# The product of (tanh + 1) with the gated value in layer 2 goes from VectorE to GpSimd, as a product and one more sum

## The chip, the cores and the metric

The kernel runs on one core of a Trainium2 chip. The metric is the device time of one execution in microseconds (us). In the profile PE is the matmul side of TensorE and PEld its weight loads, DVE is VectorE, ACT is ScalarE, POOL is GpSimd and SP is SyncE, which only issues transfers here.

## The reference, cut to what matters

Two layers run one after the other over 2048 tokens of width 256. Each adds s * silu(f) to the residual x. In layer 1 (index 0 in the reference) s is an attention and f a mixture of 64 experts; in layer 2 (index 1) s is an attention and f two ternary projections:

```python
x = L0_attn_q
xn = _layernorm(x)
s = _L0_attn_ref(xn, ...)
g = _silu(_L0_ffn_ref(xn, ...))
x = x + s * g
xn = _layernorm(x)
s = _L1_attn_ref(xn, ...)
g = _silu(_L1_ffn_ref(xn, ...))
x = x + s * g
```

The change touches the first `x = x + s * g`. The kernel computes silu(a) as a/2 * (tanh(a/2) + 1), with the factor of one half already in s. So with s0 = s/2 and a = the output of the experts, the sum is x + (tanh(a/2) + 1) * (s0 * a).

## The kernel before, in words

Tokens lie 128 to a tile, 16 tiles in all. The first 305 us are layer 1: the routing, the experts and its attention. Then a transfer brings the experts' sums back (`acc_ld`), and a software pipeline runs layer 2. It works on 8 pairs of tiles (NP = 8, GT = 2 tiles to a pair), and pair p holds tiles p and p + 8. A tensor of a pair is 128 partitions by 512 values.

Every engine runs a loop `for p in range(-AHEAD, NP)` with AHEAD = 3, and its instructions execute in the order written. In turn p of the loop the stages work on different pairs:

- pair p + 3: the end of layer 1. GpSimd adds the two halves of the experts' sum (`total`, L482) and multiplies s0 by it (`gated`, L488). ScalarE takes the tanh (`gate`, L685) into `tg`. VectorE forms (tg + 1) * s0 (`silu`, L1053). GpSimd adds that to x (`add_gated`, L493).
- pair p + 2: the layer norm. VectorE takes the moments (`moments`, L1060 to L1069). GpSimd raises the variances to the power -0.5 (`roots`, L513), for several pairs at once. VectorE mends these by a Newton step (`newton`, L1045 to L1047: three small instructions, each waiting for the one ahead) and normalises (`normalise`, L1081, two instructions, then L1083 and L1086).
- pair p + 1: the first projections and the gelu. TensorE multiplies (`fc` L1475, `qkv` L1462), ScalarE runs gelu, copy and square (`hidden`, L709, L716, L722; four times a turn), and VectorE forms the low half of the gelu's output (`low`, L1121, four times a turn) and that of x (`low_x`, L1091).
- pair p: the last projection and the sum. VectorE reduces the squares (`sum_squares`, L1128) and takes the spreads (`spreads`, L1134 to L1137, which feed `roots`), then scales (`half_scale`, L1145). TensorE multiplies (`down1`, L1508, which may start once `silu2` of the pair before has emptied its PSUM banks, and `square_sums`, L1515). ScalarE takes a tanh (`gate2`, L747), VectorE forms `silu2` (L1153) and `attended` (L1162), and GpSimd adds to x (`finish`, L507).

VectorE's order within a turn is: low_x, sum_squares, moments, spreads, low 0, newton, half_scale, normalise, products, low 1, score_difference, silu2, silu, low 2, attended, low 3. GpSimd's is: weigh, total, gated, roots, add_gated, finish. After `roots` has ended, VectorE's `newton` is released, and GpSimd goes on to `add_gated`. Turns p = -3 to -1 fill the pipeline, and the last turn with an `add_gated` is p = 4.

GpSimd's and VectorE's helper `then` issues an instruction and waits for its end on the same engine.

Of the kernel before, what the change touches and what calls it, by code (L numbers as in the profile page):

```python
# [10 lines left out]
ALU = mybir.AluOpType  # L11
# [42 lines left out]
NP = NT // 2  # L54
# [16 lines left out]
AHEAD = 3  # L71
# [6 lines left out]
def build(nc, q, router, Wkv, Wo, shared, sd, wgu_d, wdn_d, wqkv, wpo, wpo4, wfc, wpj, out):  # L78
# [9 lines left out]
    with ExitStack() as ctx:  # L88
        def sb(name, shape, dt=F32):
            return ctx.enter_context(nc.sbuf_tensor(name, shape, dt))  # L90

        def sem(name):
            return ctx.enter_context(nc.semaphore(name))
# [7 lines left out]
        x = sb("x", [P, NT, D])  # L101
# [61 lines left out]
        s0 = A[:, 4096:8192].rearrange("p (t d) -> p t d", t=NT)  # L163
# [33 lines left out]
        def l1(n):  # L197
            at[0] += n
            assert at[0] <= 10752, at
            return F[:, at[0] - n:at[0]]  # L200
# [8 lines left out]
        tg = [l1(GT * D).rearrange("p (s d) -> p s d", s=2) for _ in range(2)]  # L209
# [66 lines left out]
        acc_ready, gated_ready, gate_ready, silu_ready, x1_ready, xh_ready, xT1_ps, xT_hi_ready, xT_lo_ready = [  # L276
            sem(n) for n in ("acc_ready", "gated_ready", "gate_ready", "silu_ready", "x1_ready", "xh_ready", "xT1_ps",
                             "xT_hi_ready", "xT_lo_ready")]
# [10 lines left out]
        def pair(a, p):  # L289

            return a.rearrange("p (s i) d -> p s i d", s=2)[:, :, p, :]
# [105 lines left out]
        def _(pool):  # L397
# [91 lines left out]

            def add_gated(p):  # L490

                pool.wait_ge(silu_ready, p + 1)
                pool.tensor_tensor(pair(x, p), pair(x, p), tg[p % 2], ALU.add).then_inc(x1_ready, 1)  # L493

            def weigh(p):
# [275 lines left out]
        def _(ve):  # L771
            step = [0]

            def mark(ins):
                step[0] += 1
                ins.then_inc(dve, 1)
                return step[0]

            def then(ins):
                ve.wait_ge(dve, mark(ins))  # L780
# [259 lines left out]
            def newton(p):  # L1040

                c = root_cols(p)
                v, y, t_ = nv[:, c], ny[:, c], nt2[:, c]
                ve.wait_ge(root_ready, p + 3)
                then(ve.tensor_tensor(t_, y, y, ALU.mult))  # L1045
                then(ve.scalar_tensor_tensor(out=t_, in0=t_, scalar=-0.5, in1=v, op0=ALU.mult, op1=ALU.mult))
                then(ve.scalar_tensor_tensor(out=y, in0=t_, scalar=1.5, in1=y, op0=ALU.add, op1=ALU.mult))  # L1047

            def silu(p):

                ve.wait_ge(gate_ready, p + 1)
                ve.wait_ge(gated_ready, p + 1)
                ve.scalar_tensor_tensor(out=tg[p % 2], in0=tg[p % 2], scalar=1.0, in1=pair(s0, p), op0=ALU.add, op1=ALU.mult)\  # L1053
                    .then_inc(silu_ready, 1)

            def moments(p):

                ve.wait_ge(x1_ready, p + 1)
                for q_ in range(GT):
                    last = mark(ve.bn_stats(st1[:, q_, :], x[:, p + NP * q_, :]))  # L1060
                ve.wait_ge(dve, last)
                for q_ in range(GT):
                    last = mark(ve.bn_aggr(mv1[:, q_, :], st1[:, q_, :]))
                ve.wait_ge(dve, last)

                var = mv1[:, :, 1]
                mark(ve.tensor_scalar(nv[:, 0:GT], var, EPS_LN, None, ALU.add))
                ve.wait_ge(dve, step[0])
                ins = ve.tensor_scalar(nv[:, GT:2 * GT], var, 1.0 + EPS_Q, EPS_Q * EPS_LN, ALU.mult, ALU.add)  # L1069
                if p < 2:  # L1070
                    ins.then_inc(v_in, 1)
                    ve.wait_ge(v_in, p + 1)
                else:
                    then(ins)

            def normalise(p):

                if p >= 2:
                    ve.wait_ge(xT1_ps, p - 1)
                for q_ in range(GT):  # L1080
                    ve.tensor_scalar(xh[p % 2][:, q_, :], x[:, p + NP * q_, :], mv1[:, q_, 0:1], ny[:, GT + q_:GT + q_ + 1],  # L1081
                                     ALU.subtract, ALU.mult).then_inc(xh_ready, 1)
                then(ve.tensor_tensor(ratio[:, :], nv[:, GT:2 * GT], ny[:, GT:2 * GT], ALU.mult))  # L1083
                if p >= 2:
                    ve.wait_ge(kv_ready1, p - 1)
                ve.scalar_tensor_tensor(out=kvscale[p % 2][:, :], in0=ny[:, 0:GT], scalar=1.0 / WSCALE, in1=ratio[:, :],  # L1086
                                        op0=ALU.mult, op1=ALU.mult).then_inc(scale_ready, 1)

            def low_x(p):
                ve.wait_ge(xT_hi_ready, p + 1)  # L1090
                ve.tensor_tensor(xT_lo, bk_(0).rearrange("p (k n) -> p k n", k=KH), xT_hi, ALU.subtract)\  # L1091
                    .then_inc(xT_lo_ready, 1)
# [16 lines left out]
            def score_difference(p):  # L1109
                ve.wait_ge(prod_ready, p + 1)  # L1110
                ve.tensor_reduce(dif[:, :].rearrange("p (g r) -> p g r", r=REP1), pr, AX.X, ALU.add).then_inc(dif_ready, 1)

            def low(p, j):

                n = FC * p + j
                ve.wait_ge(hi_ready, n + 1)
                ve.wait_ge(sq_ready, n + 1)
                if p >= 2:
                    ve.wait_ge(z_ps, p - 1)
                cols = slice(512 * j, 512 * j + 512)  # L1120
                ve.tensor_tensor(loT[p % 2][:, cols], fc_bank(n), hiT[p % 2][:, cols], ALU.subtract).then_inc(lo_ready, 1)  # L1121

            def sum_squares(p):

                ve.wait_ge(sq_ready, FC * p + FC)
                if p:
                    ve.wait_ge(z_ps, p)
                ve.tensor_reduce(sq1, sq.rearrange("p (j t b) -> p t j b", j=FC, b=2), AX.XY, ALU.add).then_inc(sqsum_ready, 1)  # L1128

            def spreads(p):  # L1130

                ve.wait_ge(z_ps, p + 1)
                for q_ in range(GT):
                    last = mark(ve.tensor_scalar(st3[:, :, q_], z_bank(q_)[:, D:D + 2], 1.0 / FF1, None, ALU.mult))  # L1134
                ve.wait_ge(dve, last)
                then(ve.tensor_tensor(msq[:, :], st3[:, 0, :], st3[:, 0, :], ALU.mult))
                ve.scalar_tensor_tensor(out=nv[:, 2 * GT:3 * GT], in0=st3[:, 1, :], scalar=EPS_Q, in1=msq[:, :],  # L1137
                                        op0=ALU.add, op1=ALU.subtract).then_inc(v_in, 1)
                ve.wait_ge(v_in, p + 3)

            def half_scale(p):

                if p >= 2:
                    ve.wait_ge(ztanh_ready, GT * (p - 1))
                ve.tensor_scalar(zhalf[p % 2][:, :], ny[:, 2 * GT:3 * GT], gwc[:, 0:1], None, ALU.mult).then_inc(zhalf_ready, 1)  # L1145

            def silu2(p):

                if p:
                    ve.wait_ge(out_ready, p)  # L1150
                for q_ in range(GT):
                    ve.wait_ge(ztanh_ready, GT * p + q_ + 1)
                    ve.scalar_tensor_tensor(out=zu[:, q_, :], in0=tz[:, q_, :], scalar=1.0, in1=z_bank(q_)[:, 0:D],  # L1153
                                            op0=ALU.add, op1=ALU.mult).then_inc(zu_ready, 1)
# [20 lines left out]
            for p in range(-AHEAD, NP):  # L1175
                if 0 <= p + 1 < NP:
                    low_x(p + 1)
                if p >= 0:
                    sum_squares(p)
                if 0 <= p + 2 < NP:  # L1180
                    moments(p + 2)
                if p >= 0:
                    spreads(p)
                if 0 <= p + 1 < NP:
                    low(p + 1, 0)
                if p >= -2:
                    newton(p)
                if p >= 0:
                    half_scale(p)
                if 0 <= p + 2 < NP:  # L1190
                    normalise(p + 2)
                if 0 <= p + 1 < NP:
                    products(p + 1)
                    low(p + 1, 1)
                    score_difference(p + 1)
                if p >= 0:
                    silu2(p)
                if p + AHEAD < NP:
                    silu(p + AHEAD)
                if 0 <= p + 1 < NP:  # L1200
                    low(p + 1, 2)
                if p >= 0:
                    attended(p)
                if 0 <= p + 1 < NP:
                    low(p + 1, 3)
# [383 lines left out]
```

## Time and profile before

| | |
|---|---|
| median of 3 runs | 433.42 us (433.1 to 434.67) |
| span of the profiled execution | 433.6 us |
| PE busy over the span | 348.9 us (80%) |
| DVE busy over the span | 277.6 us (64%) |
| ACT busy over the span | 197.5 us (46%) |
| POOL busy over the span | 242.5 us (56%) |

Busy times are sums over the whole span. They mix layer 1, in which GpSimd mostly issues transfers, with layer 2, in which it computes. All times in the rows below are microseconds from the start of the span, unless marked ns. A bracket behind a row gives how long the engine stood idle ahead of it and what released it. When two instructions of one line are merged, the row carries x2 and the time for both together.

### The profile page before, as it was taken

The numbers are of one execution on the slowest core, as the hardware profiler recorded it, in microseconds if no ns is written. First come the engines' busy times: TensorE is split into PE (matmuls) and PEld (weight loads), VectorE is DVE, ScalarE is ACT, GpSimd is POOL, SyncE is SP. The second block draws the span as 40 slices with busy tenths as digits, with TensorE's granted clock in tenths as the row PEclk, the third lists the DMA queues.
The fourth block names the chain that finished last, engine by engine and source line by source line (L and its number), as shares of the span: only waits on it lengthen the run. The fifth ranks groups of instructions, "written<-read, shape, count | busy, mean of one in ns | idle before, by whom it ended". The sixth has DMA issues, their size and how long they took to land.

```text
span 433.6 us, 6895 instructions
## 1 busy us (share of the span) xinstructions
PE 348.9 (80%) x2106; PEld 274.1 (63%) x2106; DVE 277.6 (64%) x826; ACT 197.5 (46%) x493; POOL 242.5 (56%) x230
## 2 busy tenths in 40 slices
PE   0899895878899896989799987967039889888894
PEld 0894354457688666868588775755027778777773
DVE  4928997185565452545556756554257888999875
ACT  1344351362454252474244444513017876766871
POOL 6460000537878867867888888846373346654211
PEclk9999998889999997999789999869658999999998
DMA  8770005897888788897767877544760000000001
GB/s 279 276 246 14 0 1 174 259 269 183 194 195 194 169 246 230 207 270 144 185 144 182 192 147 187 93 54 44 205 201 0 2 25 26 26 25 20 9 24 50
DMA packets 37703, 58.40 MB, mean 135 GB/s; under 512 B 6091, under 2 KB 27171, under 8 KB 37283
## 3 DMA queue, kind: packets, MB, share of 16 engines
q1 hardware_dynamic: 25379, 39.08, 28.0%
q0 software_dynamic: 12288, 18.88, 24.0%
q8 instruction: 18, 0.29, 0.3%
q14 instruction: 18, 0.15, 0.1%
HBM read 40.22 MB, written 17.73 MB: 134 GB/s over the span
## 4 chain that ended last, share of the span: by engine, by line
PE 37%; DVE 24%; DMA 13%; issue 10%; ACT 7%; POOL 7%; SPq 0%; POOLq 0%; DVEq 0%; ACTq 0%
DMA W<-tok_d,idxE 7%; PE two L1389 5%; PE two L1305 4%; PE two L1341 4%; DMA acc_d<-W,idxE 4%; PE two L1401 4%; PE two L1249 4%; DVE F L1128 3%; POOL ny L513 2%; PE two L1214 2%; PE two L1378 2%; PE two L1263 2%; PE two L1316 2%; ACT W L722 2%; ACT two L709 2%
## 5 line engine op out<-in xcount | busy, mean ns | idle before, releaser
L474 POOL DMA_INDIRECT acc_d<-W,idxE x64 | 103.7, 1621 | 33.4 <-DVE W L972 19.2
L454 POOL DMA_INDIRECT W<-tok_d,idxE x56 | 56.4, 1007 | 62.9 <-DMA tok_d<-F 46.1
L1008 DVE SCALAR_TENSOR_TENSOR W<-W,two 128x88 f32<-128x88 f32 x64 | 15.6, 244 | 63.2 <-ACT W L652 63.0
L636 ACT ACTIVATE W<-two 128x256 f32<-128x256 f32 x64 | 24.4, 382 | 49.9 <-PE two L1378 49.1
L1341 PE MATMUL two<-A,v 128*128 128x128 f32 x256 | 35.9, 300 | 5.5 <-issue 5.5
L1341 PEld LDWEIGHTS two<-A,v 128*128 128x128 f32 x256 | 35.1, 215 | 7.7 <-issue 6.9
L1508 PE MATMUL two<-W,A 128*128 128x257 f16 x256 | 29.9, 273 | 10.4 <-DVE F L1153 9.9
L1378 PE MATMUL two<-ident,W 128*128 128x128 f32 x112 | 23.2, 291 | 13.8 <-DMA W<-tok_d,idxE 11.7
L1508 PEld LDWEIGHTS two<-W,A 128*128 128x128 f16 x256 | 24.0, 98 | 15.9 <-DVE F L1153 11.7
L1475 PE MATMUL two<-F,wfcT 128*128 128x256 f16 x256 | 32.6, 282 | 1.4 <-DVE F L1091 1.4
L972 DVE TENSOR_SCALAR W<-two,W 128x256 f32<-128x256 f32 x56 | 26.8, 479 | 10.0 <-PE two L1401 7.0
L1389 PE MATMUL two<-W 128*128 128x176 f32 x160 | 32.0, 324 | 0.3 <-ACT W L643 0.2
L709 ACT ACTIVATE two<-two,gwv 128x512 f32<-128x512 f32 x32 | 21.3, 664 | 23.3 <-PE two L1475 23.3
L1378 PEld LDWEIGHTS two<-ident,W 128*128 128x128 f32 x112 | 14.8, 147 | 26.5 <-DMA W<-tok_d,idxE 14.9
L1305 PE MATMUL two<-kT,vT 128*128 128x512 f32 x64 | 30.5, 597 | 0.0
L869 DVE TENSOR_REDUCE nmax<-two 128x1 f32<-128x1024 f32 x16 | 19.6, 1224 | 16.2 <-PE two L1305 16.2
L1475 PEld LDWEIGHTS two<-F,wfcT 128*128 128x128 f16 x256 | 25.0, 101 | 6.0 <-DVE F L1091 1.8
L493 POOL TENSOR_TENSOR x<-x,F 128x512 f32<-128x512 f32 x8 | 10.1, 1267 | 33.3 <-DVE F L1053 33.3
L1401 PE MATMUL two<-W 88*128 88x256 f32 x80 | 25.6, 403 | 1.1 <-DVE W L972 0.7
L1389 PEld LDWEIGHTS two<-W 128*128 128x128 f32 x160 | 25.3, 199 | 0.9 <-issue 0.9
L1121 DVE TENSOR_TENSOR A<-two,A 128x512 f16<-128x512 f32 x32 | 22.0, 686 | 3.0 <-ACT W L722 2.5
L1395 PE MATMUL two<-ident,W 128*88 128x128 f32 x64 | 18.3, 286 | 5.2 <-DVE W L1010 5.2
(221 smaller groups left out, 830.3 us busy)
## 6 DMA issues: line engine op xcount, KB each, us to landing
W<-in_gu SPq DMA_DIRECT2D x20, 352.0 KB
F<-in_gu SPq DMA_DIRECT2D x12, 352.0 KB
acc_d<-xn SPq DMA_DIRECT2D x8, 512.0 KB, 4.4
W<-in_dn SPq DMA_DIRECT2D x20, 176.0 KB
F<-in_dn SPq DMA_DIRECT2D x12, 176.0 KB
x<-in_q SPq DMA_DIRECT2D x4, 512.0 KB, 6.9
A<-in_Wo SPq DMA_DIRECT2D x1, 2048.0 KB, 13.1
tok_d<-xn SPq DMA_DIRECT2D x4, 512.0 KB, 4.3
```

The lines of the kernel that those rows point to most:

```text
L454: pool.indirect_dma_start(out=xg[n % XR], out_offset=None, in_=tok_d[:, :], in_offset=bass.IndirectOffsetOnAxis(ap=idxE[:, n:n + 1], axis=0))\
L474: pool.indirect_dma_start(out=acc_d[n % 2][:, :], out_offset=bass.IndirectOffsetOnAxis(ap=idxE[:, n:n + 1], axis=0), in_=ysb[n % YS], in_o ...
L636: sc.activation(xgT[n % 2], bk_(2)[:, 0:D].rearrange("p (k n) -> p k n", k=KH), ACT.Copy)\
L709: sc.activation(fc_bank(n), fc_bank(n), ACT.Gelu, scale=gwv[:, 0:1]).then_inc(gelu_ready, 1)
L972: ve.tensor_scalar(ysb[n % YS], bk_(3)[:, 0:D], xg[n % XR][:, D + n:D + n + 1], 0.5, ALU.mult, ALU.mult)\
L1305: ins = pe.matmul(two[2][:, 512 * h:512 * h + 512], vT[:, rows], kT[:, at:at + 512], start=True, stop=True)
L1341: ins = pe.matmul(bk_(1)[:, 0:P], v[:, (ORDER[t] // NP) * NP + i, :], probT[t % 2][:, i, :], start=(i == 0), stop=(i == 7))
L1378: ins = pe.transpose(bk_(2)[:, P * k:P * k + P], xg[n % XR][:, P * k:P * k + P], ident[:, :])
L1389: ins = pe.matmul(gu[n % 2], xgT[n % 2][:, k, :], wgu[r][:, n % WG, k, :], start=(k == 0), stop=(k == KH - 1))
L1401: pe.matmul(bk_(3)[:, 0:D], hT[n % 2], wdn[(n // WG) % WR][:, n % WG, :], start=True, stop=True)\
L1475: ins = pe.matmul(to, wfcT[:, k, P * c:P * c + P], part[:, k, :], start=(i == 0), stop=(i == 3))
L1508: pe.matmul(z_bank(q_)[:, 0:D + 1], part[p % 2][:, at:at + P], wpj2[:, c, 0:D + 1], start=(c == 0 and part is hiT), stop=(c == FF1 // P - ...
```

## The change

For every pair but the first, VectorE's `silu` is no longer issued. GpSimd's `add_gated` does its work in three instructions in place of one: it adds s0 (which holds s0 * a by then) to x, multiplies `tg` (the tanh) by s0 in place, and adds the product to x. Each waits for the one ahead. The wait for `silu_ready` becomes one for `gated_ready` ahead of the first sum and one for `gate_ready` (ScalarE's tanh) ahead of the product. Pair 0 is unchanged.

```diff
             def add_gated(p):
 
-                pool.wait_ge(silu_ready, p + 1)
+                if p == 0:
+                    pool.wait_ge(silu_ready, 1)
+                else:
+                    pool.wait_ge(gated_ready, p + 1)
+                    then(pool.tensor_tensor(pair(x, p), pair(x, p), pair(s0, p), ALU.add))
+                    pool.wait_ge(gate_ready, p + 1)
+                    then(pool.tensor_tensor(tg[p % 2], tg[p % 2], pair(s0, p), ALU.mult))
                 pool.tensor_tensor(pair(x, p), pair(x, p), tg[p % 2], ALU.add).then_inc(x1_ready, 1)
...
                 if p >= 0:
                     silu2(p)
-                if p + AHEAD < NP:
-                    silu(p + AHEAD)
+                if p + AHEAD == 0:
+                    silu(0)
                 if 0 <= p + 1 < NP:
                     low(p + 1, 2)
```

## Rows read from the trace of the kernel before

**Rows 1.** Windows, five turns: span; busy PE, PEld, DVE, ACT, POOL; granted clock

```profile
338.68:403.66 64.98, 57.23 (x478) 47.99 (x475) 59.49 (x166) 48.18 (x101) 32.26 (x28) 1.00 0.07 22
```

**Rows 2.** Timeline of POOL, turn p = 2 and the later root steps

```profile
364.68 1.33 POOL L513 TENSOR_TENSOR ny<-nv,expo 128x6 f32<-128x6 f32 x1 [0.96 <-DVE nv L1137]
370.85 1.27 POOL L493 TENSOR_TENSOR x<-x,F 128x512 f32<-128x512 f32 x1 [4.84 <-DVE F L1053]
372.24 1.27 POOL L507 TENSOR_TENSOR x<-x,F 128x512 f32<-128x512 f32 x1
...
403.66 1.33 POOL L513 TENSOR_TENSOR ny<-nv,expo 128x6 f32<-128x6 f32 x1 [3.55 <-DVE nv L1137]
...
416.05 0.71 POOL L513 TENSOR_TENSOR ny<-nv,expo 128x2 f32<-128x2 f32 x1 [3.59 <-DVE nv L1137]
```

**Rows 3.** Timeline of DVE, turn p = 2

```profile
366.05 0.17 DVE L1045 TENSOR_TENSOR nt<-ny 128x6 f32<-128x6 f32 x1 [0.72 <-POOL ny L513]
...
366.65 0.23 DVE L1145 TENSOR_SCALAR zhalf<-ny,gwc 128x2 f32<-128x2 f32 x1
366.79 0.73 DVE L1081 TENSOR_SCALAR F<-x,mv,ny 128x256 f32<-128x256 f32 x2
...
369.43 0.74 DVE L1153 SCALAR_TENSOR_TENSOR F<-F,two 128x256 f32<-128x256 f32 x2
370.09 0.69 DVE L1053 SCALAR_TENSOR_TENSOR F<-F,A 128x512 f32<-128x512 f32 x1
...
371.29 0.87 DVE L1162 SCALAR_TENSOR_TENSOR F<-two,zhalf,F 128x256 f32<-128x256 f32 x2
372.07 0.68 DVE L1121 TENSOR_TENSOR A<-two,A 128x512 f16<-128x512 f32 x1
```

**Rows 4.** Timeline of PE, turn p = 2

```profile
370.23 3.71 PE L1508 MATMUL two<-W,A 128*128 128x257 f16 x32 [1.55 <-DVE F L1153]
```

**Rows 5.** Timeline of DVE, turn p = 6, which has no moments and no silu

```profile
415.35 0.23 DVE L1134 TENSOR_SCALAR st<-two 128x2 f32<-128x2 f32 x2 [1.43 <-PE two L1515]
```

**Rows 6.** Timeline of ACT, turn p = 2

```profile
365.59 0.65 ACT L685 ACTIVATE F<-xn 128x512 f32<-128x512 f32 x1
...
370.52 0.64 ACT L722 ACTIVATE W<-two 128x512 f32<-128x512 f32 x1
```

**Rows 7.** Timeline of POOL in turns p = -2 and -1

```profile
317.41 1.05 POOL L513 TENSOR_TENSOR ny<-nv,expo 128x4 f32<-128x4 f32 x1
320.85 1.27 POOL L493 TENSOR_TENSOR x<-x,F 128x512 f32<-128x512 f32 x1 [2.39 <-DVE F L1053]
...
323.48 1.27 POOL L488 TENSOR_TENSOR A<-A,xn 128x512 f32<-128x512 f32 x1
```

**Rows 8.** Timeline of DVE in turns p = -2 and -1, and L1069 in p = 5

```profile
318.56 0.16 DVE L1045 TENSOR_TENSOR nt<-ny 128x4 f32<-128x4 f32 x1 [2.26 <-POOL ny L513]
...
319.16 0.73 DVE L1081 TENSOR_SCALAR F<-x,mv,ny 128x256 f32<-128x256 f32 x2
...
323.67 1.11 DVE L1069 TENSOR_SCALAR nv<-mv 128x2 f32<-128x2 f32 x1
...
402.76 0.17 DVE L1069 TENSOR_SCALAR nv<-mv 128x2 f32<-128x2 f32 x1
```

**Rows 9.** Timeline of DVE at the start of layer 1

```profile
13.92 1.38 DVE L788 TENSOR_SCALAR xn<-x,mv,rstd 128x256 f32<-128x256 f32 x4
...
17.89 3.22 DVE L788 TENSOR_SCALAR xn<-x,mv,rstd 128x256 f32<-128x256 f32 x4
```

**Rows 10.** Timeline of POOL beside it: the first of 14 sums

```profile
17.82 0.72 POOL L446 TENSOR_TENSOR WoS<-WoS,A 128x256 f32<-128x256 f32 x1
```

**Rows 11.** The same timeline: all 14 together

```profile
17.82 11.16 POOL L446 TENSOR_TENSOR WoS<-WoS,A 128x256 f32<-128x256 f32 x14
```

**Rows 12.** Windows about the change of layers and at the end, columns as in rows 1

```profile
304.00:308.00 4.00, 0.00 (x0) 0.00 (x0) 1.67 (x1) 0.00 (x0) 0.06 (x1) 0.98 0.35 46
308.00:312.00 4.00, 0.00 (x0) 0.00 (x0) 0.00 (x0) 0.63 (x1) 1.83 (x2) 0.50 0.93 284
427.00:434.00 7.00, 0.75 (x4) 0.32 (x2) 3.01 (x10) 0.84 (x2) 0.36 (x1) 0.77 0.11 37
```

## Prediction

> **What bounds the kernel now.** I read the chain of waits first, to find who sets the pace of layer 2, then the timelines of VectorE and GpSimd side by side over one turn, and last the places where the two compute at the same moment. Layer 1 isn't touched, so only the time after 305 us can move.
>
> Five turns of layer 2, from the root step of pair 0 to that of pair 5, last 64.98 us, 13.00 us each, and VectorE is busy for 59.49 of them [rows 1]. Most of what it lacks is the wait for the root step on GpSimd, 0.72 us a turn [rows 3]. So VectorE with that one step sets the pace. TensorE is close behind. It starts the last projection only when silu2 has emptied its banks (1.55 us idle, released by L1153) [rows 4]. In turn 6, where VectorE has less to do, it waits 1.43 us for TensorE [rows 5]. The roots at 403.66 and 416.05 are 12.39 us apart there [rows 2], which I take as TensorE's floor for a turn. GpSimd has room: after the roots (364.68 + 1.33 = 366.01) it stands idle for 4.84 us until silu is done [rows 2]. The reader is to see that this gap is where the new work goes, and to look at what VectorE does in it.
>
> **What is removed.** One silu of 0.69 us on VectorE in each of the turns -2 to 4. The next starts before it has ended. From 370.09 to 371.29 VectorE passes silu and a low of the same shape [rows 3], so each is worth 1.20 / 2 = 0.60 us of its time. Without anything else a turn would take 13.00 - 0.60 = 12.40 us, just above TensorE's 12.39. ScalarE allows it nearly: its last square ends at 370.52 + 0.64 = 371.16 [rows 6], and the low that needs it starts at 372.07 now and would start at 371.47. In turns -2 and -1 the silu lies in time in which VectorE waits, and saves nothing.
>
> **What is added.** Two more instructions of 128 x 512 on GpSimd. A sum there takes 1.27 us [rows 2] and a product 1.27 us [rows 7]. Between two that wait for each other, 14 sums of 0.72 us took 11.16 us, 0.80 us each [rows 10, 11], so 0.08 us passes between them. Three in a row take 3 x 1.27 + 2 x 0.08 = 3.97 us. The tanh that the second needs ends at 365.59 + 0.65 = 366.24 [rows 6], the first sum at about 367.28, so that wait costs nothing. GpSimd would be done at 366.01 + 3.97 = 369.98, ahead of the 372.12 of now, and `finish` still waits for VectorE. On GpSimd's own queue the step is free: behind it stand only `finish`, then `weigh`, `total`, `gated` and the next roots, and none comes later by it.
>
> **What is moved, and into what.** The one sum of now runs beside `attended` and the last `low`, which take one operand from PSUM; they take 0.87 us for two and 0.68 us [rows 3]. The three of afterwards run from 366.01 to 369.98. There VectorE has its three Newton instructions (366.05 on), half_scale and two normalisations, all from SBUF to SBUF [rows 3]. How do such instructions fare beside a GpSimd sum or product? Two places show it. L1069, 2 values to a partition, takes 0.17 us alone, and 1.11 us in turn -1. It started at 323.67 and ended at 324.78, and GpSimd's product ran from 323.48 to 324.75 [rows 7, 8]. And the normalisations of layer 1, of the form of L1081, take 1.38 us for four alone and 3.22 us for four beside the GpSimd sums [rows 9]. That is 0.80 us each, one for each sum. The last ended at 17.89 + 3.22 = 21.11, and the fourth sum at 17.82 + 4 x 0.80 - 0.08 = 20.94, so 0.17 us behind it [rows 9, 10, 11]. VectorE's small instructions stand still until GpSimd's has ended, and pass one at a time.
>
> No row shows the Newton instructions (tensor by tensor, both from SBUF) beside such a GpSimd instruction. From below, they pass freely (nothing). From above, they are held like L1069. I take the upper value, since they are nearest to L1069: as small, and with no operand in PSUM, while the ones that pass freely have one. The Trainium skill (SBUF — State Buffer, "Who interferes with whom") says that a VectorE instruction with two inputs in SBUF contends with a GpSimd instruction that reads SBUF, and that the one which starts first holds the shared port to its end. By it the Newton instructions are held, which gives the forecast below; were that part of it wrong, the sum would be that of the first rival. This case's trace has no row on two such inputs, while the held L1069 agrees with it (1.11 us).
>
> The cost of a turn then: GpSimd's first sum starts as the roots end, together with the first Newton instruction. Each of the three Newton steps waits for the one ahead, so each is held by one GpSimd instruction. The third ends with the third of GpSimd, at 369.98 + 0.03, and half_scale starts at about 370.05 in place of 366.65: 3.40 us late. If two of them slip through one gap between GpSimd's instructions, the normalisations are held instead, and it is about 3.0 us. All that VectorE does after this is in its own order, so nothing hides it. TensorE's floor moves with it, since it starts after silu2, and ScalarE waits for half_scale too. A turn takes 12.40 + 3.40 = 15.80 us. Five of them: 79.0 - 65.0 = 14.0 us more (12.0 with 3.0 us).
>
> In the filling of the pipeline, turn -2 has the same collision: roots end at 317.41 + 1.05 = 318.46, and the three GpSimd instructions at 322.43. The normalisations start at about 322.50 in place of 319.16 [rows 7, 8], on the path to TensorE's first matmul of layer 2: 3.3 us. Turn -1 has one as well, yet VectorE waits for ScalarE in that turn more than once, and I cost it at nothing; without that cover it would be some 1 to 2 us. Turns 5 to 7 have no add_gated and stay.
>
> The sum: 14.0 + 3.3 = 17.3 us on a span of 433.6 us makes 450.9. The median stands 0.2 us under the profiled span, so I predict 451 us. Its own range is 448 to 454, from 3.0 us a turn to the open cost of turn -1.
>
> **The rivals.**
>
> - Only the tensor_scalar forms are held, not the Newton steps. half_scale ends with GpSimd's first instruction, the first normalisation with the second and the second normalisation with the third, at 369.98 + 0.17 = 370.15 in place of 366.79 + 0.73 = 367.52 [rows 3]. That is 2.63 us a turn: 5 x (12.40 + 2.63 - 13.00) = 10.2 us, and in turn -2 the pair ends with the second GpSimd instruction, 318.46 + 2.62 + 0.17 = 321.25 in place of 319.89, 1.4 us. Total 11.6, so 445 us. For it: rows exist for this form alone.
> - The same, but half_scale and the first normalisation, between which there is no wait, slip through one gap. The second ends at 366.01 + 2.62 + 0.17 = 368.80, 1.28 us late: 5 x 0.68 = 3.4 and 1.4 in turn -2, so 438 us. Against it: four normalisations with no wait between them passed one for each sum [rows 9].
> - The other side: nothing of this is held. The change then gives its 0.60 us in five turns, held back a little by TensorE's floor and ScalarE: 5 x 0.55 = 2.7 us, so 430.8 us. It decides if the delay at the Newton steps and normalisations together is under 0.60 us a turn. For it: VectorE is the bound and GpSimd is idle. Against it: L1069 and the four normalisations. If a delay near 0.6 us cancels the gain, there is no change.
> - TensorE's clock falls. With turns of 15.8 us its idle time grows by about 2.8 us a turn. In the trace the granted clock is 1.00 through the five turns [rows 1]. With TensorE idle it is still 0.98 in the mean from 304 to 308, 0.50 (the 1.2 GHz level) from 308, and 0.77 in the mean over the last 7 us [rows 12]. If it fell for a part of each turn, the 3.71 us of the last projection [rows 4] would be doubled there, and the result would be some 10 to 18 us more, 461 to 469 us. Against it: the added idle time is split, part of it ahead of the transposes, which wait for the normalisations, and part ahead of the last projection.
>
> **How the numbers follow.** Chances: the forecast 0.60, the first rival 0.17, the second 0.09, nothing held 0.07, a cancelling delay 0.03, the clock 0.04. The range of 438 to 455 holds the forecast, the first rival and the second at its edge. A measurement of this kernel can tell about 0.5% from no change. Slower: 0.60 + 0.17 + 0.09 + 0.04 = 0.90, less 0.02 for what I may have missed, 0.88. Faster 0.07, within 0.5% 0.05.
>
> **What would show it.** In the timeline of a middle turn: no L1053; three GpSimd instructions back to back right behind the roots; Newton instructions of about 1.3 us each in place of 0.17; half_scale some 3.4 us later behind the roots' end; roots 15.8 us apart. Newton at 0.17 and L1081 stretched would be the first rival. The prediction is wrong if VectorE's instructions keep their lengths there, or if GpSimd is the one to be held.

## The result, and the profile after

| | before | after |
|---|---|---|
| median | 433.26 us (4 runs) | 461.02 us (4 runs) |
| profiled span | 433.6 us | 458.7 us |
| five turns of layer 2, root step of pair 0 to that of pair 5 | 64.98 us | 86.82 us |
| granted TensorE clock in them | 1.00 | 0.88 |

The ratio of the times is 1.0636, with a 95% interval of 1.0579 to 1.0693. The direction was as forecast, the size wasn't: 461 us lies above the range of 438 to 455. The executions of the changed kernel took 459.22 to 464.72 us, and the profiled one is that of 460.46. Its span, from the first instruction to the last, is 1.8 us shorter than its time, and so it is for every other run here of which both are known (1.7 to 1.8 us). The span of 433.6 before therefore belongs to an execution of about 435.3 us by estimate, some 2 us longer than the median. What follows explains the difference of the two profiled spans, 25.1 us, and not the whole 27.8 us between the medians.

GpSimd's timeline of the changed kernel, with the same steps as in rows 2 (L519 is the root step, and L496, L498 and L499 are the three instructions of add_gated):

```profile
341.98 1.33 POOL L519 TENSOR_TENSOR ny<-nv,expo 128x6 f32<-128x6 f32 x1 [1.66 <-DVE nv L1143]
...
377.16 1.33 POOL L519 TENSOR_TENSOR ny<-nv,expo 128x6 f32<-128x6 f32 x1 [2.70 <-DVE nv L1143]
378.47 1.27 POOL L496 TENSOR_TENSOR x<-x,A 128x512 f32<-128x512 f32 x1
379.81 1.28 POOL L498 TENSOR_TENSOR F<-F,A 128x512 f32<-128x512 f32 x1
381.17 1.26 POOL L499 TENSOR_TENSOR x<-x,F 128x512 f32<-128x512 f32 x1
...
394.38 1.33 POOL L519 TENSOR_TENSOR ny<-nv,expo 128x6 f32<-128x6 f32 x1 [2.68 <-DVE nv L1143]
...
428.80 1.33 POOL L519 TENSOR_TENSOR ny<-nv,expo 128x6 f32<-128x6 f32 x1 [5.33 <-DVE nv L1143]
```

The three stand right behind the roots and keep their lengths of before. They take 3.96 us together (378.47 to 382.43; forecast 3.97), and the next roots come 17.2 us later in place of 13.0.

VectorE's timeline of the same turn, where rows 3 have that of before (L1051 to L1053 are Newton, L1151 is half_scale, L1087 normalise, L1159 silu2, L1140 the spreads):

```profile
378.53 1.23 DVE L1051 TENSOR_TENSOR nt<-ny 128x6 f32<-128x6 f32 x1 [0.72 <-POOL ny L519]
379.79 0.17 DVE L1052 SCALAR_TENSOR_TENSOR nt<-nt,nv 128x6 f32<-128x6 f32 x1
379.99 1.12 DVE L1053 SCALAR_TENSOR_TENSOR ny<-nt,ny 128x6 f32<-128x6 f32 x1
381.15 1.30 DVE L1151 TENSOR_SCALAR zhalf<-ny,gwc 128x2 f32<-128x2 f32 x1
382.37 0.73 DVE L1087 TENSOR_SCALAR F<-x,mv,ny 128x256 f32<-128x256 f32 x2
...
385.00 0.74 DVE L1159 SCALAR_TENSOR_TENSOR F<-F,two 128x256 f32<-128x256 f32 x2
...
393.68 0.23 DVE L1140 TENSOR_SCALAR st<-two 128x2 f32<-128x2 f32 x2 [1.76 <-PE two L1521]
```

Read the lengths against GpSimd's ends. Newton 1 ends at 379.76, with L496 at 379.74. Newton 2 starts at 379.79, 0.02 us ahead of L498, and passes in 0.17 us. Newton 3 ends with L498. Half_scale starts 0.02 us ahead of L499 (381.15 and 381.17), and yet it is held and ends with it. All five turns show the same four lengths within 0.01 us. Normalise starts 382.37 - 378.49 = 3.88 us behind the roots' end, in place of 366.79 - 366.01 = 0.78 [rows 2, 3]: 3.10 us late.

The last line is new. VectorE, which was the bound, stands idle for 1.76 us until TensorE has finished the square sums. TensorE's timeline, where rows 4 have 3.71 us and 1.55 us idle:

```profile
347.96 0.66 PE L1455 MATMUL two<-ident,F 128*128 128x128 f32 x4 [2.43 <-DVE F L1087]
350.61 6.12 PE L1514 MATMUL two<-W,A 128*128 128x257 f16 x32 [1.99 <-DVE F L1159]
...
383.15 0.66 PE L1455 MATMUL two<-ident,F 128*128 128x128 f32 x4 [1.98 <-DVE F L1087]
385.80 5.36 PE L1514 MATMUL two<-W,A 128*128 128x257 f16 x32 [1.99 <-DVE F L1159]
```

And windows of 2 us of the later stretch, with that of the five turns below them (busy PE, PEld, DVE, ACT and POOL, then the granted clock):

```profile
384.00:386.00 2.00, 0.20 (x2) 0.19 (x3) 2.00 (x6) 1.97 (x4) 0.00 (x0) 1.00 0.00 0
386.00:388.00 2.00, 2.00 (x13) 1.50 (x12) 2.00 (x5) 1.38 (x4) 0.80 (x1) 0.59 0.00 0
388.00:390.00 2.00, 2.00 (x12) 1.42 (x11) 2.00 (x2) 0.00 (x0) 2.00 (x3) 0.56 0.28 93
390.00:392.00 2.00, 2.00 (x21) 1.78 (x19) 1.82 (x7) 0.00 (x0) 1.55 (x2) 1.00 0.12 38
...
341.98:428.80 86.82, 66.50 (x471) 52.36 (x468) 71.84 (x161) 47.65 (x100) 44.75 (x38) 0.88 0.05 16
```

TensorE waited twice, 1.98 us for normalise and 1.99 us for silu2, with four short transposes between. The last projection began at 385.80, still at 2.4 GHz. The clock fell to 1.2 GHz about half a microsecond later and came back shortly before 390, by the shares in the windows. The same 32 matmuls took 1.65 us more. From silu2 to the square sums the path runs through TensorE alone, so this delay is paid in full: a turn of 17.21 us, beside 15.56 with the clock held up (e3_keep_clock below). The first of the five turns is longer, 17.97 us. In it TensorE waited 2.43 us for normalise, and the projection took 6.12 us.

In the filling of the pipeline one more collision appears. GpSimd and then VectorE in turn -2:

```profile
309.34 1.26 POOL L482 TENSOR_TENSOR xn<-xn,F 128x512 f32<-128x512 f32 x1 [6.06 <-DMA F<-acc_d]
...
317.76 1.25 POOL L496 TENSOR_TENSOR x<-x,A 128x512 f32<-128x512 f32 x1
...
321.66 1.31 POOL L482 TENSOR_TENSOR xn<-xn,F 128x512 f32<-128x512 f32 x1
323.11 1.26 POOL L488 TENSOR_TENSOR A<-A,xn 128x512 f32<-128x512 f32 x1
```

```profile
319.27 1.11 DVE L1053 SCALAR_TENSOR_TENSOR ny<-nt,ny 128x4 f32<-128x4 f32 x1
320.42 2.70 DVE L1087 TENSOR_SCALAR F<-x,mv,ny 128x256 f32<-128x256 f32 x2
...
323.22 1.17 DVE L1092 SCALAR_TENSOR_TENSOR kvscale<-ny,ratio 128x2 f32<-128x2 f32 x1
```

GpSimd goes from add_gated straight to total and gated of the next pair, and so the two normalisations take 2.70 us in place of 0.73 [rows 8] and end with total (321.66 + 1.31), not with the last of the three. L1092 is held by gated in turn, but that costs nothing here, since VectorE then still waits 0.62 us for ScalarE.

### The profile page after: what moved, and what is told of

Same layout as the page of the kernel before. It is cut to its first block, busy times and chain, and to the rows that moved or that the text cites. A ratio compares the mean times of both kernels' runs of the same rounds, so it can differ in the third digit from the quotient of the medians.

```text
span 458.7 us, 6902 instructions
## 1 busy us (share of the span) xinstructions
PE 357.1 (78%) x2106; PEld 277.5 (60%) x2106; DVE 292.0 (64%) x819; ACT 197.0 (43%) x493; POOL 259.9 (57%) x244
## 4 chain that ended last, share of the span: by engine, by line
PE 45%; DVE 18%; issue 12%; POOL 11%; DMA 7%; ACT 5%; POOLq 0%; DVEq 0%; SPq 0%; ACTq 0%
PE two L1514 7%; PE two L1395 4%; DMA W<-tok_d,idxE 4%; PE two L1311 4%; PE two L1347 4%; PE two L1407 4%; PE two L1255 3%; PE two L1481 3%; PE two L1220 3%; POOL acc_d L474 3%; POOL ny L519 2%; POOL W L454 2%; PE two L1384 2%; PE two L1269 2%; DMA acc_d<-W,idxE 2%
## 5 line engine op out<-in xcount | busy, mean ns | idle before, releaser
L1514 PE MATMUL two<-W,A 128*128 128x257 f16 x256 | 38.8, 324 | 12.2 <-DVE F L1159 11.6
L1514 PEld LDWEIGHTS two<-W,A 128*128 128x128 f16 x256 | 29.0, 116 | 21.7 <-DVE F L1159 13.4
L1347 PE MATMUL two<-A,v 128*128 128x128 f32 x256 | 34.5, 293 | 5.6 <-issue 5.6
L1347 PEld LDWEIGHTS two<-A,v 128*128 128x128 f32 x256 | 33.7, 208 | 7.7 <-issue 6.9
L1455 PE MATMUL two<-ident,F 128*128 128x128 f32 x32 | 5.6, 300 | 31.1 <-DVE F L1087 31.1
L513 POOL TENSOR_TENSOR x<-x,F 128x512 f32<-128x512 f32 x7 | 8.9, 1265 | 34.9 <-DVE F L1168 34.9
L519 POOL TENSOR_TENSOR ny<-nv,expo 128x6 f32<-128x6 f32 (+2 forms) x10 | 11.5, 1148 | 27.4 <-DVE nv L1143 24.7
L1407 PE MATMUL two<-W 88*128 88x256 f32 x80 | 25.1, 396 | 1.1 <-DVE W L978 0.7
```

The source lines that it names most:

```text
L1347: ins = pe.matmul(bk_(1)[:, 0:P], v[:, (ORDER[t] // NP) * NP + i, :], probT[t % 2][:, i, :], start=(i == 0), stop=(i == 7))
L1407: pe.matmul(bk_(3)[:, 0:D], hT[n % 2], wdn[(n // WG) % WR][:, n % WG, :], start=True, stop=True)\
L1514: pe.matmul(z_bank(q_)[:, 0:D + 1], part[p % 2][:, at:at + P], wpj2[:, c, 0:D + 1], start=(c == 0 and part is hiT), stop=(c == FF1 // P - ...
```

## The experiments

All are compared with the kernel before, run on the same chip. Where a turn is given, it is the distance of the root steps of pairs 0 to 5 divided by five, as in rows 1.

**The same three instructions, later (e1_after_norm).** One wait more:

```diff
                     pool.wait_ge(gated_ready, p + 1)
+                    pool.wait_ge(scale_ready, p)
                     then(pool.tensor_tensor(pair(x, p), pair(x, p), pair(s0, p), ALU.add))
```

> The changed kernel, with the three GpSimd instructions of every pair but the first held back until VectorE has done its normalisation (one wait on scale_ready ahead of the first). They then run beside VectorE instructions that take an operand from PSUM. Theory (VectorE's SBUF-only instructions stand still beside a GpSimd sum or product): Newton back at 0.17 us, half_scale 0.87 us behind the roots' end, a turn at 12.4 to 12.5 us, clock 1.00, 430 to 432 us. Rival (three instructions on GpSimd are too many wherever they stand, since they delay finish, weigh and the next roots): little better than 461 us, 455 or more.

Measured: ratio 0.9947, interval 0.9910 to 0.9984. VectorE's timeline, GpSimd's and the window of the five turns:

```profile
366.45 0.17 DVE L1052 TENSOR_TENSOR nt<-ny 128x6 f32<-128x6 f32 x1 [0.72 <-POOL ny L520]
...
367.19 0.73 DVE L1088 TENSOR_SCALAR F<-x,mv,ny 128x256 f32<-128x256 f32 x2
...
376.32 0.76 DVE L1074 TENSOR_SCALAR nv<-mv 128x2 f32<-128x2 f32 x1
```

```profile
368.32 1.27 POOL L497 TENSOR_TENSOR x<-x,A 128x512 f32<-128x512 f32 x1 [1.91 <-DVE kvscale L1093]
...
375.77 1.28 POOL L488 TENSOR_TENSOR A<-A,xn 128x512 f32<-128x512 f32 x1 [0.44 <-POOL xn L482]
```

```profile
339.85:403.09 63.24, 56.35 (x471) 48.14 (x468) 57.63 (x161) 47.38 (x100) 44.74 (x39) 1.00 0.07 22
```

The collision is gone, the clock is 1.00, and a turn takes 12.65 us, 0.35 less than before the change. The same work at another moment costs nothing where it cost 25 us, and by this measurement it wins about 0.5%. A turn isn't 12.40 us, because gated now holds L1074 of the moments. Behind the root step the moments come 0.59 us earlier than before the change (351.09 - 339.85 = 11.24, before 350.51 - 338.68 = 11.83), and gated only 0.37 us. L1074 takes 0.76 us in the turn shown, which lasts 12.93, 0.45 in three others, and 0.17 in the last, beside which no gated runs. The rival, that three instructions are too many wherever they stand, falls.

**One instruction in the collision (e2_one_more).** From the kernel before, only the sum with s0 is added behind the roots; VectorE keeps a product of 0.68 us:

```diff
+                if p:
+                    pool.wait_ge(gated_ready, p + 1)
+                    then(pool.tensor_tensor(pair(x, p), pair(x, p), pair(s0, p), ALU.add))
                 pool.wait_ge(silu_ready, p + 1)
...
-                ve.scalar_tensor_tensor(out=tg[p % 2], in0=tg[p % 2], scalar=1.0, in1=pair(s0, p), op0=ALU.add, op1=ALU.mult)\
-                    .then_inc(silu_ready, 1)
+                if p:
+                    ve.tensor_tensor(tg[p % 2], tg[p % 2], pair(s0, p), ALU.mult).then_inc(silu_ready, 1)
...
```

> The kernel before, with only the sum x + s0 put on GpSimd right behind the roots; VectorE still forms the product tanh * s0, and GpSimd adds it as before. One GpSimd instruction meets Newton in place of three. Theory (one small VectorE instruction waits for each GpSimd instruction): first Newton instruction 1.2 us, the others 0.17, a turn 13.0 + 1.1 = 14.1 us, clock 1.00, 1.1 us more in turn -2: about 440 us. Rival (most of the loss is the fallen clock, and comes only when TensorE stands long): a turn within 0.3 us of 13.0, 434 us.

Measured: ratio 1.0215, interval 1.0175 to 1.0254, median 443.52 us. VectorE's timeline and the windows of two turns:

```profile
370.70 1.23 DVE L1048 TENSOR_TENSOR nt<-ny 128x6 f32<-128x6 f32 x1 [0.72 <-POOL ny L516]
371.97 0.17 DVE L1049 SCALAR_TENSOR_TENSOR nt<-nt,nv 128x6 f32<-128x6 f32 x1
```

```profile
355.28:369.34 14.06, 12.07 (x105) 10.07 (x103) 12.96 (x34) 10.10 (x22) 8.18 (x8) 1.00 0.06 20
369.34:384.53 15.19, 12.79 (x90) 9.94 (x88) 12.96 (x34) 9.13 (x20) 8.18 (x7) 0.89 0.06 18
```

One GpSimd instruction holds one Newton instruction, and a turn with full clock takes 14.06 us, as the theory had it (14.1); the other two turns with full clock took 14.36 and 14.01. But in two of the five turns the clock fell to 0.89 in the mean and they took 14.95 and 15.19 us, which the expectation missed. So a delay of 1.06 us is enough to bring the clock down in some turns. TensorE's timeline of one turn in which it fell, and of one in which it didn't:

```profile
375.95 5.36 PE L1514 MATMUL two<-W,A 128*128 128x257 f16 x32 [2.00 <-DVE F L1159]
...
405.50 3.71 PE L1514 MATMUL two<-W,A 128*128 128x257 f16 x32 [1.99 <-DVE F L1159]
```

**The clock kept up (e3_keep_clock).** The changed kernel with unused matmuls in TensorE's two waits:

```diff
+            def filler(bank, n):
+                for _ in range(n):
+                    pe.matmul(bk_(bank)[:, 0:P], ident16[:, :], ones16[:, :], start=True, stop=True)
...
             for p in range(-1, NP):
+                if 1 <= p <= 5:
+                    filler(0, 24)
                 if p + 1 < NP:
                     turn_x(p + 1)
+                if 1 <= p <= 5:
+                    pe.wait_ge(prod_ready, p + 1)
+                    filler(1, 24)
```

> The changed kernel, with 24 matmuls of 128 columns into a free part of PSUM put into each of TensorE's two waits of turns 1 to 5, so that it doesn't stand idle. They compute nothing that is used. Theory (standing VectorE instructions cost 3.1 us a turn, and the fallen clock, which stretches L1514 from 3.71 to 5.36 us, another 1.7): clock near 1.00, turns at 12.4 + 3.1 = 15.5 us, 5 x 1.7 = 8.5 us less than the changed kernel, about 452 us. Rival (the clock's fall is covered by VectorE's standing still): turns stay at 17.2 us, 461 us, or grow by the fillers.

Measured: ratio 1.0396, interval 1.0318 to 1.0474, median 451.38 us. TensorE's timeline and the window of the five turns:

```profile
382.81 1.51 PE L1526 MATMUL two<-ones,ident 128*128 128x128 f16 x24 [0.41 <-DVE F L1112]
384.39 3.69 PE L1514 MATMUL two<-W,A 128*128 128x257 f16 x32
```

```profile
344.62:422.43 77.81, 71.68 (x710) 61.62 (x708) 71.99 (x161) 47.74 (x100) 44.87 (x39) 1.00 0.06 19
```

With more work on TensorE the kernel is faster than the changed one: by about 10 us in the times, with two executions here, and by 86.82 - 77.81 = 9.0 us in the five turns. The clock stays at 1.00, L1514 is back at 3.69 us and a turn takes 15.56 us. VectorE's Newton and half_scale are held as in the changed kernel. This splits the loss of a turn: 15.56 - 13.00 = 2.56 us from the held instructions less silu, and 17.36 - 15.56 = 1.80 us from the clock. The 1.80 is a mean: about 1.65 us in each of four turns, and 2.41 in the first.

**GpSimd writes and reads nothing (e4_only_write).** From the kernel before:

```diff
+        junk = W[:, 0:684].bitcast(F16)
...
+                if p:
+                    for _ in range(3):
+                        then(pool.memset(junk, 0.0))
                 pool.wait_ge(silu_ready, p + 1)
```

> The kernel before, with three memsets (128 x 1370, fp16) on GpSimd right behind the roots, for every pair but the first; they write a free tile and read nothing. By a memset of 1024 that took 0.95 us each should take about 1.27 us. Rival (any GpSimd instruction holds them): Newton 1.1 to 1.2 us, 3.1 us a turn on top of 13.0 and the clock falls, 455 to 465 us. Second rival (writes hold nothing): 433 us.

Measured: ratio 1.0208, interval 1.0153 to 1.0264, median 443.25 us. GpSimd's and VectorE's timelines (L1049 is the first Newton instruction, L1149 half_scale, L1085 normalise):

```profile
370.82 3.89 POOL L495 MEMSET W<- 128x1368 f16 x3
```

```profile
370.90 0.17 DVE L1049 TENSOR_TENSOR nt<-ny 128x6 f32<-128x6 f32 x1 [0.72 <-POOL ny L517]
...
371.50 0.58 DVE L1149 TENSOR_SCALAR zhalf<-ny,gwc 128x2 f32<-128x2 f32 x1
371.64 1.90 DVE L1085 TENSOR_SCALAR F<-x,mv,ny 128x256 f32<-128x256 f32 x2
```

The same 3.9 us of GpSimd, and Newton passes freely beside it, while the tensor_scalars are held (0.58 us for 0.23, 1.90 us for 0.73). So there are two ways of being held. An instruction with two inputs in SBUF waits for a GpSimd instruction that reads; a tensor_scalar from SBUF to SBUF waits for one that only writes, too. Two turns take 14.17 us, 1.17 more than before, by which the two normalisations end later; two others with full clock take 14.46 and 14.10. In the one that is left the clock fell here too:

```profile
384.00:399.29 15.29, 12.57 (x87) 9.67 (x85) 13.06 (x34) 8.83 (x19) 10.67 (x10) 0.89 0.05 18
```

**The delay without its cause (e6_stall_only).** e1_after_norm, with VectorE busy for 3.1 us by itself:

```diff
                 if p >= -2:
                     newton(p)
+                if 0 <= p <= 4:
+                    then(ve.tensor_reduce(nmax[:, 0:1], kT[:, :], AX.X, ALU.add))
+                    then(ve.tensor_reduce(nmax[:, 1:2], vT[:, 0:650], AX.X, ALU.add))
```

> e1_after_norm, in which GpSimd meets none of VectorE's SBUF-only instructions of the normalisation, with two reductions of dead tiles (3.1 us together, results unused) put on VectorE between Newton and half_scale in turns 0 to 4. This is the delay of the changed kernel without its cause. Theory (a turn of the changed kernel is 12.4 + 3.1 us of delay, and the fallen clock adds the rest): the clock falls below 1.00 and L1514's counterpart is stretched to 5 us, turns at 17.2 us, 433 + 5 x 4.2 = 452 to 455 us. Rival (GpSimd's port also costs something beyond VectorE's delay, or the clock fell for another reason): clock 1.00 and turns at 15.5 to 15.7 us, 445 to 448 us.

Measured: ratio 1.0586, interval 1.0505 to 1.0667, median 459.81 us. VectorE's timeline, TensorE's, and the window of the five turns:

```profile
379.64 2.29 DVE L1196 TENSOR_REDUCE nmax<-kT 128x1 f32<-128x2048 f32 x1
381.96 0.83 DVE L1197 TENSOR_REDUCE nmax<-vT 128x1 f32<-128x650 f32 x1
```

```profile
386.40 5.36 PE L1518 MATMUL two<-W,A 128*128 128x257 f16 x32 [2.00 <-DVE F L1160]
```

```profile
342.33:429.53 87.20, 66.34 (x471) 52.25 (x469) 73.20 (x171) 47.72 (x100) 44.71 (x38) 0.88 0.05 16
```

The turns of the changed kernel come back without any collision behind the roots: 17.44 us each beside 17.36, the same clock of 0.88, the same 5.36 us. The turns are near the 17.2 us of the theory, the total is above its 452 to 455. The five turns took 22.2 us more than before, where the theory had 21, and in the profiled execution layer 2 began 3.5 us later (its first sum of `total` at 313.57, before at 310.03). These turns show no cost of GpSimd's contention beyond VectorE's delay, and the delay alone brings down the clock.

**A version to keep (e5_late_three_on, and e1_again beside it).** As e1_after_norm, with pairs 1 and 2 left to VectorE:

```diff
-                if p == 0:
-                    pool.wait_ge(silu_ready, 1)
+                if p < 3:
+                    pool.wait_ge(silu_ready, p + 1)
...
-                if p + AHEAD == 0:
-                    silu(0)
+                if p + AHEAD < 3:
+                    silu(p + AHEAD)
```

> As e1_after_norm, with the work of pairs 1 and 2 left on VectorE as before the change, so that only pairs 3 to 7 go to GpSimd, after the normalisation. Theory (in turns -2 and -1 VectorE waits anyway, so silu there costs nothing, and GpSimd needs 2.7 us less for x of those pairs): the same turns of 12.6 us as in e1_after_norm, 0 to 0.7 us better than it, 430.5 to 432 us beside 433.3 for the kernel before. Rival (the order in e1_after_norm is what helped the filling): 0.5 us worse than it.

> e1_after_norm again in more rounds beside e5_late_three_on. Expected by its first trace: about 1.8 us under the kernel before (five turns of 12.65 in place of 13.00), a ratio of 0.996.

Measured: e5_late_three_on 0.9972 (0.9939 to 1.0006), e1_again 0.9976 (0.9944 to 1.0008). Neither is told apart from the kernel before by these times, and not from each other. In the traces, the stretch from the first sum of `total` to the root step of pair 5 takes 403.66 - 310.03 = 93.6 us before the change, 402.47 - 310.78 = 91.7 in e1_again, and 400.82 - 309.90 = 90.9 in e5_late_three_on. The five turns take 12.65 us each in e1_again and 12.59 in e5_late_three_on, and the filling is 0.5 us shorter in the latter (337.87 - 309.90 = 27.97 beside 339.24 - 310.78 = 28.46). So late placement wins 2 to 3 us in layer 2 of a profiled execution, while the executions of the kernel before beside them ranged from 431.42 to 438.82 us. The first measurement of the same kernel gave 0.9947. That late placement is a little faster than the kernel before is likely but not shown, and its size isn't settled.

## Why the prediction was right in direction and wrong in size

- **What bounds the kernel, and TensorE close behind.** Right. VectorE with the root step set the pace. What I didn't carry further: TensorE's path from silu2 to the square sums had next to no slack, so whatever slowed TensorE would be paid in full. In e3_keep_clock the square sums end at 390.49 and VectorE takes them at 390.61.
- **The removed silu, 0.60 us.** Right. e1_after_norm has turns of 12.65 us, and the missing 0.25 is L1074, held: less what it takes beyond its 0.23 us of before, four turns last 12.39 to 12.40 us, and the fifth, without gated, 12.46.
- **The added instructions, 3.97 us on GpSimd.** Right (3.96), and with no cost to GpSimd's own queue: e1_after_norm.
- **SBUF-to-SBUF instructions stand still, 3.40 us a turn.** Right in kind: Newton, of which no row existed, is held (1.23 and 1.12 us). The size was 3.10 us, near the lower of the two values given, because Newton 2 passes; the third to be held is then half_scale, which the forecast had free (it starts 2.66 us behind the roots' end and takes 1.30). The rivals in which only the tensor_scalars are held, or nothing is, fall. What the Trainium skill says of two inputs in SBUF (SBUF — State Buffer, "Who interferes with whom") is borne out: Newton took 1.23 us beside a GpSimd instruction that reads, and 0.17 us beside one that only writes.
- **A turn takes 15.80 us.** This is the step that failed. It kept TensorE's clock at 1.00, and put the cost of a fallen clock at nothing. The fallen clock stood among the rivals, with a chance of 0.04 and a price of 10 to 18 us on top of the forecast. It came, in every one of the five turns, and cost 9.0 us, a little under that price. With the clock held up a turn takes 15.56 us, as that sum would have it within 0.3; with the clock as it fell, 17.36. I argued that the idle time is split in two and so harmless. It was split as I said, 1.98 and 1.99 us, and the clock fell all the same. No row spoke for the argument either: those with a low clock had one long idle stretch in them [rows 12], and none showed two waits of 2 us close together.
- **The filling, 3.3 us.** Under-sized: 341.98 - 309.34 = 32.64 us from the first sum to the root step of pair 0, before 338.68 - 310.03 = 28.65, so 4.0 us. The missing part is total, which follows at once and holds the second normalisation: the two end 3.9 us later behind the roots than before. Turn -1 costs nothing, as forecast. The sum of `total` from which 28.65 counts, in the kernel before:

```profile
310.03 1.25 POOL L482 TENSOR_TENSOR xn<-xn,F 128x512 f32<-128x512 f32 x1 [5.96 <-DMA F<-acc_d]
```

The account of the profiled spans: the five turns 86.82 - 64.98 = 21.84 us, of which 5 x 2.56 = 12.8 are the held instructions less silu and 5 x 1.80 = 9.0 the clock (by e3_keep_clock); the filling 4.0; the start of layer 2, 0.7 us earlier in this execution; the end no different. Together 25.1 us. The forecast had 14.0 and 3.3, and the runs show 12.8 and 4.0 for these two, 16.8 beside 17.3. So nearly all that was missing is the clock. Of the 27.8 us between the medians, the other 2.7 are no effect shown here: by the estimate above the profiled execution before was about 2 us longer than its median, and the profiled one after 0.6 us shorter than its own. The forecast put the time 0.2 us under the span, where every pair of the two shows it 1.7 or 1.8 us above; since both kernels have the same offset, this doesn't bear on the difference.

Open: what decides whether the clock falls. In e2_one_more TensorE waited 2.0 us ahead of L1514 in all five turns. In three of them it also waited 0.40 us ahead of the transposes; the clock fell in two of these three. In e4_only_write it waited 2.0 us in all five, too, with 0.50 us ahead of the transposes in three, and the clock fell in one of these.

## What to carry to other kernels

Before work is moved to GpSimd, look at which VectorE instructions run at that moment, and not only at GpSimd's idle time. Beside GpSimd's sums and products here, instructions with two inputs in SBUF and tensor_scalars from SBUF to SBUF stood still, however short they are; of those that came behind the roots only Newton 2 passed. Those with an operand in PSUM didn't, and nor did the reductions and the batch-norm statistics, though they read SBUF. One wait that shifts the same GpSimd work by 2 us took away the whole loss of 25 us. And when a delay on one engine makes TensorE wait, price its clock too: here 3.1 us of delay in a turn cost 4.9.

## What the runs showed of the hardware that I had not expected

- In four of the five turns the clock fell although no single wait of TensorE was longer than 2.0 us (1.98 and 1.99 us with 0.66 us of transposes between), and in e2_one_more after waits of 0.40 and 2.00 us. 48 unused matmuls a turn, 3.0 us, took 9.0 us off the five turns.
- GpSimd's memsets, which read nothing, hold VectorE's tensor_scalars but not its instructions with two inputs. The memsets themselves took 3.89 us for three.
- The batch-norm statistics, SBUF to SBUF, aren't held: two take 0.74 us in the changed kernel right beside gated, and 0.74 us at 325.62, where GpSimd is idle. A reduction of 128x2048 isn't either: 2.27 us at 388.24 beside GpSimd's weigh, total and gated, and 2.29 us in e6_stall_only with GpSimd idle.

```profile
390.43 0.74 DVE L1066 BATCH_NORM_STATS2 st<-x 128x6 f32<-128x256 f32 x2
```

```profile
390.42 1.27 POOL L488 TENSOR_TENSOR A<-A,xn 128x512 f32<-128x512 f32 x1
```

- Of the four instructions Newton 1 to 3 and half_scale, three were held. Newton 2 began in the gap between two GpSimd instructions (379.74 to 379.81), 0.02 us before its end, and passed. Half_scale began as early in the next gap and was held for 1.30 us. Newton 2 has two inputs in SBUF and half_scale is a tensor_scalar; whether that makes the difference no run here tested.
